# Third expert layer of a GNN and mixture-of-experts kernel: 512-column products with both weight halves, two running sums a token, bias terms on GpSimd

## The chip, the cores and the metric

The kernel runs on one core of a Trainium2 chip. The metric is the device time of one execution in microseconds (us). Before the change three runs gave 3012.4 us as the median (3011.11 to 3012.64).

## What is computed

A graph layer is followed by a dense mixture of eight experts over all 6250 rows of 256 features. The change touches only the second part, and in it the last product:

```python
h = jnp.einsum('bfd,edh->bfeh', x, W1) + b1
h = jax.nn.relu(_bn(h, g1, be1, m1, v1))
h = jnp.einsum('bfeh,ehk->bfek', h, W2) + b2
h = jax.nn.relu(_bn(h, g2, be2, m2, v2))
y = jnp.einsum('bfeh,ehd->bfed', h, Wo) + bo
return jnp.einsum('bfed,fe->bfd', y, w)      # w: softmax over the 8 experts
```

Every row goes through every expert. Products are done in split form: each operand is a rounded high half (fp32r) and a low half, and high x high, low x high and high x low are summed.

## The kernel before, in words

A first part (about 2110 us) normalizes, gathers 200000 edges, takes a segment maximum and runs the graph layer's products. The expert part follows. It has 7 chunks (c) of 7 token tiles (t) of 128 rows, and 8 experts (e) a chunk: 56 steps, n = 8c + e, written out one after another.

TensorE runs L2(n), L1(n+1), L3(n) in a step, so that what follows L3(n) is L2(n+1). L1 and L2 (lines 202 to 204) have the weights as the stationary operand and write a block m of 896 columns (a 512 and a 384 piece) into PSUM banks 0 and 1 (m = 0) or 2 and 3 (m = 1). ScalarE evacuates each block: `av` with scale, bias and Relu (line 1707), then the rounded copy `h1h` or `h2h` (line 1709). VectorE subtracts the two to get the low half, `low` (line 1846), which has two SBUF inputs. L2 waits until both blocks of `h1l` are there, L3 until both of `h2l` are there.

L3 (products on lines 2024 to 2026) has the tokens as the stationary operand. For each token tile and each of the two k blocks it does three products of 256 columns: h2h x high weights, h2l x high weights, h2h x low weights. Four token pairs go in turn to banks 4 and 5, so pair i waits until VectorE has read pair i-2.

VectorE runs its work in a hand-written order. Its part of L3 is `weighted` (line 1854): y = ps * w + y, 256 elements for each of 7 token tiles. `biased` (line 1841) adds the bias row times the weight: y = bo * w + y, also 7 a step, with both tensor inputs in SBUF. Chunk c+1 is prepared meanwhile: transposes on TensorE (lines 1928, 1939), `x_one`, `measure`, `norm`, `norm_lo`, router logits (`logits_in`, line 1819 on) and `softmax` on VectorE.

GpSimd has nothing in this part but one accumulating DMA a chunk (line 1648). SyncE issues the weights three steps ahead (`weights`), the chunk's residual rows and the output; the latter waits for `s_acc`, the count of `weighted` done.

## Time and profile before

| | us |
|---|---|
| median of three runs | 3012.4 |
| the profiled execution, its own time | 3013.89 |
| its span, first to last instruction | 3012.1 |
| expert part in the trace | about 2111 to 3012 |

The span is the time on the chip between the first and the last instruction that the profiler recorded; about 1.8 us of the execution's own time lie around it. Busy shares of the span are 93% for TensorE matmuls, 76% for VectorE, 65% for ScalarE, 49% for GpSimd, all of GpSimd's in the first part. A step of the expert part takes 14.84 us where nothing of the next chunk is prepared. A row of the timeline gives start, length, engine, line and operands; matmuls overlap, so the distance between two starts is their price, not the length.

### The profile page before, as it was taken

The numbers are of one execution on the slowest core, as the hardware profiler recorded it, in microseconds if no ns is written. First come the engines' busy times: TensorE is split into PE (matmuls) and PEld (weight loads), VectorE is DVE, ScalarE is ACT, GpSimd is POOL, SyncE is SP. The second block draws the span as 40 slices with busy tenths as digits, with TensorE's granted clock in tenths as the row PEclk, the third lists the DMA queues.
The fourth block names the chain that finished last, engine by engine and source line by source line (L and its number), as shares of the span: only waits on it lengthen the run. The fifth ranks groups of instructions, "written<-read, shape, count | busy, mean of one in ns | idle before, by whom it ended". The sixth has DMA issues, their size and how long they took to land. (4 is left out here: it accounts for less than half of the span.)

```text
span 3012.1 us, 40449 instructions
## 1 busy us (share of the span) xinstructions
PE 2796.6 (93%) x14193; PEld 2342.5 (78%) x14193; DVE 2292.7 (76%) x4785; ACT 1943.0 (65%) x2661; POOL 1484.6 (49%) x1550
## 2 busy tenths in 40 slices
PE   6699999999999999999999998789899999999998
PEld 6577777777776777777777777678799999999998
DVE  6887888888787888887878774498677677676766
ACT  5577777777777777777777765416465565655554
POOL 3677777777777777777777777631000000000000
PEclk9899999999999999999999999899899999999999
DMA  8577777777776666676666666411324334243231
GB/s 252 176 265 231 252 244 244 247 238 247 247 246 233 227 221 224 231 229 223 226 222 222 227 207 214 161 53 75 105 105 142 121 111 136 106 142 117 105 116 56
DMA packets 165632, 560.92 MB, mean 186 GB/s; under 512 B 31278, under 2 KB 68950, under 8 KB 149428
## 3 DMA queue, kind: packets, MB, share of 16 engines
q1 hardware_dynamic: 88164, 356.25, 32.9%
q0 software_dynamic: 77264, 202.08, 23.2%
q8 instruction: 112, 1.84, 0.2%
q14 instruction: 92, 0.75, 0.1%
HBM read 321.21 MB, written 237.00 MB: 185 GB/s over the span
## 5 line engine op out<-in xcount | busy, mean ns | idle before, releaser
L698 POOL DMA_INDIRECT ring<-runs,src_i x1436 | 1386.9, 966 | 469.1 <-issue 365.6
L1162 PE MATMUL ps<-oh,zhl 128*128 128x512 f32 x3136 | 1288.8, 411 | 115.7 <-ACT oh L727 103.4
L1164 PE MATMUL ps<-oh,zhl 128*128 128x512 f32 x3136 | 1245.4, 397 | 0.0
L914 DVE SCALAR_TENSOR_TENSOR ring<-ring,pen,ps 128x256 f32<-128x256 f32 x1260 | 598.8, 475 | 303.9 <-ACT ps L739 286.9
L1162 PEld LDWEIGHTS ps<-oh,zhl 128*128 128x128 f32 x3136 | 602.5, 192 | 284.8 <-ACT oh L727 130.6
L1164 PEld LDWEIGHTS ps<-oh,zhl 128*128 128x128 f32 x3136 | 602.8, 192 | 118.8
L921 DVE TENSOR_SCALAR oh<-ps,nodef 128x512 fp32r<-128x512 f32 x896 | 667.6, 745 | 0.0
L739 ACT ACTIVATE ps<-ring 128x512 f32<-128x512 f32 x630 | 370.4, 588 | 310.7 <-DMA ring<-runs,src_i 287.2
L721 ACT ACTIVATE oh<-ids,nodeneg 128x512 fp32r<-128x512 f32 x672 | 455.9, 711 | 27.0 <-PE ps L1164 26.9
L1707 ACT ACTIVATE av<-ps,vecs 128x896 f32<-128x896 f32 x224 | 246.4, 1100 | 325.3 <-PE ps L204 325.3
L727 ACT ACTIVATE oh<-oh,ones 128x1024 fp32r<-128x1024 f32 x448 | 414.7, 926 | 1.9
L1846 DVE TENSOR_TENSOR h2l<-av,h2h 128x896 fp32r<-128x896 f32 x112 | 122.2, 1092 | 148.4 <-ACT h2h L1709 148.1
L2024 PE MATMUL ps<-fw,h2h 128*128 128x256 f32 x784 | 224.5, 286 | 3.4 <-DVE h2l L1846 3.3
L2025 PE MATMUL ps<-fw,h2l 128*128 128x256 f32 x784 | 222.2, 283 | 0.0
L2026 PE MATMUL ps<-fw,h2h 128*128 128x256 f32 x784 | 222.0, 283 | 0.0
L1648 POOL DMA_DIRECT2D y<-in_x x5 | 8.4, 1685 | 412.1 <-DMA y<-res_d 412.1
L1854 DVE SCALAR_TENSOR_TENSOR y<-ps,wv,y 128x256 f32<-128x256 f32 x392 | 168.7, 478 | 52.6 <-PE ps L2026 52.5
L914 DVE SCALAR_TENSOR_TENSOR ring<-ring,pen 128x256 f32<-128x256 f32 x304 | 146.3, 481 | 76.0 <-DMA ring<-runs,src_i 70.9
L1841 DVE SCALAR_TENSOR_TENSOR y<-bo,wv,y 128x256 f32<-128x256 f32 x392 | 173.6, 479 | 1.4 <-issue 0.2
L202 PE MATMUL ps<-h1h,fw 128*128 128x512 f32 x448 | 168.0, 375 | 2.7 <-DVE h1l L1846 2.7
L203 PE MATMUL ps<-hnl,fw 128*128 128x512 f32 x448 | 164.7, 368 | 0.0
L204 PE MATMUL ps<-hnh,fw 128*128 128x512 f32 x448 | 164.6, 367 | 0.0
(294 smaller groups left out, 3976.1 us busy)
## 6 DMA issues: line engine op xcount, KB each, us to landing
runs<-ring SPq DMA_DIRECT2D x170, 768.0 KB, 3.9
fw<-wsp SPq DMA_DIRECT2D x56, 1536.0 KB, 6.5
runs<-ring SPq DMA_DIRECT2D x68, 1024.0 KB, 4.6
ring<-runs,src_i POOLq DMA_INDIRECT x1436, 3.7
ids<-srcT_d SPq DMA_DIRECT2D x32, 256.0 KB, 5.5
res_d<-x_all SPq DMA_DIRECT2D x7, 896.0 KB
y<-res_d SPq DMA_DIRECT2D x7, 896.0 KB, 8.1
part<-in_Wx SPq DMA_DIRECT2D x16, 384.0 KB, 7.1
```

Source lines behind the costliest of these rows:

```text
L698: pool.indirect_dma_start(ring[:, k, :], None, runs[0:N, :], bass.IndirectOffsetOnAxis(ap=src_i[:, STEPS * i + k:STEPS * i + k + 1], axis= ...
L721: return act.activation(oh[:, hot(i, g, v), :], ids[:, bass.ds(h, 1), :].rearrange("p a n -> p (a n)"), ACT.Abs, bias=nodeneg[:, bass.ds(S ...
L727: act.activation(oh[:, slots, :], oh[:, slots, :].bitcast(F32), ACT.Relu, bias=ones[:, 0:1], scale=-1.0).then_inc(s_oha, 1)
L739: act.activation(ps[:, RAWB[J % 2], :], ring[:, k:k + 2, :].rearrange("p s n -> p (s n)"), ACT.Copy).then_inc(s_cp, 1)
L914: dve.scalar_tensor_tensor(out=ring[:, k, :], in0=ring[:, before, :], scalar=pen[:, STEPS * i + k:STEPS * i + k + 1], in1=row, op0=ALU.add ...
L921: dve.tensor_scalar(oh[:, hot(i, g, v), :], ps[:, IDB, :], nodef[:, SLOTS * g + v:SLOTS * g + v + 1], None, ALU.is_equal).then_inc(s_ohd, 1)
L1162: pe.matmul(ps[:, two + k, :], z_hi(g)[:, v, cols], oh[:, hot(i, g, v), :], start=g == 0 and v == 0, stop=False, skip_group_check=True)
L1164: r = pe.matmul(ps[:, two + k, :], z_lo(g)[:, v, cols], oh[:, hot(i, g, v), :], start=False, stop=False, skip_group_check=True)
L1707: act.activation(av[:, m, :], block_banks(m), ACT.Relu, bias=dv(bi, 2 * e + m), scale=dv(sc, 2 * e + m)).then_inc(s_ev, 1)
L2024: pe.matmul(o, h2h[:, k, st], fw[:, b, 0, 2, k, :], start=k == 0, stop=False)
L2025: pe.matmul(o, h2l[:, k, st], fw[:, b, 0, 2, k, :], start=False, stop=False)
L2026: r = pe.matmul(o, h2h[:, k, st], fw[:, b, 1, 2, k, :], start=False, stop=k == KC - 1)
```

## The change

L3 does, for each token tile and k block, one product of 512 columns (h2h x high and low weights side by side, written to the two halves of a whole PSUM bank) and one of 256 columns (h2l x high weights, added to the first half). Seven tiles use banks 4, 5, 0, 1, 4, 2, 3. Banks 0 to 3 are shared with L1 and L2, so L3 waits for ScalarE's evacuation of them (`s_ev`), and L2 waits for VectorE's: block 0 until tiles 0 to 3 are read, block 1 until all 7 are.

`weighted` works on 512 elements in one instruction: first half into y[c % 3], second half into a new fourth buffer y[3]. The bias terms leave VectorE. GpSimd computes bo * w into y[3] (e = 0) or into `bw` (e > 0), and then adds `bw` to y[3] tile by tile, each add after the tile's `weighted` of the step before. At the end of a chunk GpSimd adds y[3] to y[c % 3] (`finished`), and the output DMA waits for that; in the last step VectorE does these adds (`finished_last`). GpSimd's accumulating DMA for chunk c+2 is issued after expert 2 of chunk c.

```diff
-                    for i, (t0, t1) in enumerate(PAIRS):
-                        if i >= 2:
-                            pe.wait_ge(s_acc, n * TPC + PAIRS[i - 2][1])
...
-                            for k in range(KC):
-                                pe.matmul(o, h2h[:, k, st], fw[:, b, 0, 2, k, :], start=k == 0, stop=False)
-                                pe.matmul(o, h2l[:, k, st], fw[:, b, 0, 2, k, :], start=False, stop=False)
-                                r = pe.matmul(o, h2h[:, k, st], fw[:, b, 1, 2, k, :], start=False, stop=k == KC - 1)
+                    for t in range(TPC):
+                        if t == 0 and n:
+                            pe.wait_ge(s_acc, (n - 1) * TPC + 5)
+                        if t == 2:
+                            pe.wait_ge(s_ev, 4 * first + 1)
+                        if t == 4:
+                            pe.wait_ge(s_acc, n * TPC + 1)
+                        if t == 5:
+                            pe.wait_ge(s_ev, 4 * first + 3)
+                        o = ps[:, OUTBANK[t], :].rearrange("p (a n) -> p a n", a=2)
+                        for k in range(KC):
+                            pe.matmul(o, h2h[:, k, st], fw[:, b, :, 2, k, :], start=k == 0, stop=False)
+                            r = pe.matmul(o[:, 0, :], h2l[:, k, st], fw[:, b, 0, 2, k, :], start=False, stop=k == KC - 1)
                         r.then_inc(s_l3, 1)
```
```diff
                 def L2(n):
                     pe.wait_ge(s_hl6, 4 * n + 2)
                     for m in range(KC):
+                        if n:
+                            pe.wait_ge(s_acc, (n - 1) * TPC + (4, TPC)[m])
                         layer(n, 1, m, h1h, h1l)
```
```diff
+                def biased(n, t):
+                    ...
+                    if e == 0:
+                        pool.tensor_scalar(y[:, 3, t, :], bo[:, 0, :], w, None, ALU.mult).then_inc(s_bi, 1)
+                    else:
+                        pool.wait_ge(s_bi, (n - 1) * TPC + t + 1)
+                        pool.tensor_scalar(bw[:, t, :], bo[:, e, :], w, None, ALU.mult).then_inc(s_bw, 1)
+                def add_biased(n, t):
+                    pool.wait_ge(s_bw, TPC * (n - c - 1) + t + 1)
+                    pool.wait_ge(s_acc, (n - 1) * TPC + t + 1)
+                    pool.tensor_tensor(y[:, 3, t, :], y[:, 3, t, :], bw[:, t, :], ALU.add).then_inc(s_bi, 1)
+                def finished(c, t):
+                    pool.wait_ge(s_acc, (NE * c + NE - 1) * TPC + t + 1)
+                    pool.tensor_tensor(y[:, c % 3, t, :], y[:, c % 3, t, :], y[:, 3, t, :], ALU.add).then_inc(s_fin, 1)
```
```diff
-                def weighted(n, i):
+                def weighted(n, t):
-                    dve.wait_ge(s_l3, n * NPAIR + i + 1)
-                    dve.wait_ge(s_bi, n * TPC + PAIRS[i][1])
+                    dve.wait_ge(s_l3, n * TPC + t + 1)
+                    dve.wait_ge(s_bi, n * TPC + t + 1)
+                    dve.scalar_tensor_tensor(out=both(c, t), in0=ps[:, OUTBANK[t], :].rearrange("p (a n) -> p a n", a=2),
+                                             scalar=wv[:, c % 2, t * NE + e:t * NE + e + 1], in1=both(c, t),
+                                             op0=ALU.mult, op1=ALU.add).then_inc(s_acc, 1)
```

VectorE's order in a step becomes: low h2l (two blocks), low h1l block 0, weighted 0 and 1, low h1l block 1, weighted 2 and 3, (expert 7: `logits_in`), weighted 4, 5, 6, then what prepares the next chunk. In the last step it is: weighted 0 to 3; then finished_last(t-4) and weighted(t) for t = 4, 5, 6; then finished_last 3 to 6.

## Rows read from the trace of the kernel before

**Rows 1.** The page, part 1: busy time, share of span, instructions.
```profile
PE 2796.6 (93%) x14193; PEld 2342.5 (78%) x14193; DVE 2292.7 (76%) x4785; ACT 1943.0 (65%) x2661; POOL 1484.6 (49%) x1550
```
**Rows 2.** Windows: stretch, its length, then PE, PEld, DVE, ACT, POOL busy, PEclk, DMA.
```profile
2430.00:2490.00 60.00, 60.00 (x372) 55.84 (x371) 43.79 (x85) 37.24 (x38) 0.00 (x0) 1.00 0.30 106
```
**Rows 3.** Waits, 2135 to 3013 us: who waited for whom, total, times, longest.
```profile
PE ps L202 <- DVE h1l L1846: 2.7, 1, 2.7
```
**Rows 4.** Groups by line and form, whole span: VectorE reading 512 elements from PSUM.
```profile
L921 DVE TENSOR_SCALAR oh<-ps,nodef 128x512 fp32r<-128x512 f32 x896 | 667.6, 745 | 0.0
```
**Rows 5.** Timeline, TensorE, one plain step of the last chunk: start, length, operation.
```profile
2941.42 0.28 PE L2024 MATMUL ps<-fw,h2h 128*128 128x256 f32 x1
...
2946.44 0.47 PE L202 MATMUL ps<-h1h,fw 128*128 128x512 f32 x1
2946.75 0.40 PE L203 MATMUL ps<-h1l,fw 128*128 128x512 f32 x1
...
2951.40 0.39 PE L202 MATMUL ps<-hnh,fw 128*128 128x512 f32 x1
...
2952.79 0.33 PE L202 MATMUL ps<-hnh,fw 128*128 128x384 f32 x1
```
**Rows 6.** Timeline, VectorE, the same step, L3 and the start of L2.
```profile
2941.35 1.09 DVE L1846 TENSOR_TENSOR h1l<-av,h1h 128x896 fp32r<-128x896 f32 x1 [0.55 <-ACT h1h L1709]
...
2944.49 0.88 DVE L1854 SCALAR_TENSOR_TENSOR y<-ps,wv,y 128x256 f32<-128x256 f32 x2 [0.46 <-PE ps L2026]
2945.28 1.08 DVE L1846 TENSOR_TENSOR h1l<-av,h1h 128x896 fp32r<-128x896 f32 x1
2946.28 1.26 DVE L1854 SCALAR_TENSOR_TENSOR y<-ps,wv,y 128x256 f32<-128x256 f32 x3
```
**Rows 7.** Timeline, TensorE, the start of L2 in the second step.
```profile
2157.12 0.40 PE L202 MATMUL ps<-h1h,fw 128*128 128x512 f32 x1
2157.36 0.40 PE L203 MATMUL ps<-h1l,fw 128*128 128x512 f32 x1
```
**Rows 8.** Timeline, VectorE, just before that start.
```profile
2155.70 1.08 DVE L1846 TENSOR_TENSOR h1l<-av,h1h 128x896 fp32r<-128x896 f32 x1
```
**Rows 9.** Timeline, ScalarE, the step of rows 5: the second block's high half.
```profile
2942.80 0.95 ACT L1709 ACTIVATE h1h<-av 128x896 fp32r<-128x896 f32 x1
```
**Rows 10.** Timeline, GpSimd in the first 30 us: next to VectorE, and alone.
```profile
18.54 0.76 POOL L414 TENSOR_SCALAR x_all<-x_all,fine 128x256 f32<-128x256 f32 x1 [1.38 <-DVEq L490]
...
19.28 1.10 POOL L414 TENSOR_SCALAR x_all<-x_all,fine 128x256 f32<-128x256 f32 x1
...
21.05 3.99 POOL L426 TENSOR_TENSOR x_all<-x_all,h0c 128x1792 f32<-128x1792 f32 x1
27.59 0.56 POOL L414 TENSOR_SCALAR x_all<-x_all,fine 128x256 f32<-128x256 f32 x1 [2.56 <-DVEq L490]
```
**Rows 11.** Timeline, VectorE in the same microseconds.
```profile
18.23 0.17 DVE L489 SCALAR_TENSOR_TENSOR fine<-fine 128x7 f32<-128x7 f32 x1
...
18.66 0.29 DVE L539 CAST b1h<-b1r 128x256 fp32r<-128x256 f32 x1
18.86 0.58 DVE L540 TENSOR_SCALAR bb<-b1r,ident 128x256 fp32r<-128x256 f32 x1
19.36 0.67 DVE L542 TENSOR_TENSOR w1l<-w1r,w1h 128x512 fp32r<-128x512 f32 x1
...
20.68 2.02 DVE L495 TENSOR_TENSOR h0l<-ps,h0h 128x1792 fp32r<-128x1792 f32 x1
```
**Rows 12.** Timeline, VectorE, a step of expert 7: the router logits.
```profile
2514.01 0.27 DVE L1819 TENSOR_REDUCE wv<-ps 128x56 f32<-128x112 f32 x1
...
2514.79 1.26 DVE L1854 SCALAR_TENSOR_TENSOR y<-ps,wv,y 128x256 f32<-128x256 f32 x3
```
**Rows 13.** Timeline, VectorE, the end of the last step.
```profile
3003.89 0.88 DVE L1854 SCALAR_TENSOR_TENSOR y<-ps,wv,y 128x256 f32<-128x256 f32 x2 [0.56 <-PE ps L2026]
3005.32 1.27 DVE L1854 SCALAR_TENSOR_TENSOR y<-ps,wv,y 128x256 f32<-128x256 f32 x3 [0.56 <-PE ps L2026]
```

More of the change, by code:

```diff
@@ L1596, in build, with both @@
         LAST = NCH - 1
[L1597 to L1598 removed]
+        OUTBANK = (4, 5, 0, 1, 4, 2, 3)
+        def both(c, t):
+            return y[:, c % 3:4:3 - c % 3, t, :]
         def cols67(n):
@@ L1644, in _, with plus_input @@
                 pool.memset(br[:], 0.0).then_inc(s_z, 1)
-                for c in range(1, NCH):
+                def plus_input(c):
                     pool.wait_ge(s_res[c % 3], 16 * (c // 3 + 1))
@@ L1653, in _ @@
                         pool.dma_start(y[0:TAIL, c % 3, TPC - 1, :], io["x"][N - TAIL:N, :], accum_op=ALU.add).then_inc(s_rx[c % 3], 16)
+                def biased(n, t):
+                    c, e = divmod(n, NE)
+                    w = wv[:, c % 2, t * NE + e:t * NE + e + 1]
+                    if e == 0:
[4 more added lines that the diff above has]
+                def add_biased(n, t):
+                    c, e = divmod(n, NE)
+                    pool.wait_ge(s_bw, TPC * (n - c - 1) + t + 1)
[4 more added lines that the diff above has]
+                    pool.tensor_tensor(y[:, c % 3, t, :], y[:, c % 3, t, :], y[:, 3, t, :], ALU.add).then_inc(s_fin, 1)
+                plus_input(1)
+                plus_input(2)
+                pool.wait_ge(s_bo, 16)
+                for c in range(NCH):
+                    if c:
+                        pool.wait_ge(s_fin, TPC * c)
+                    pool.wait_ge(s_w, c + 1)
+                    for e in range(NE):
+                        for t in range(TPC):
+                            biased(NE * c + e, t)
+                        if e:
+                            for t in range(TPC):
+                                add_biased(NE * c + e, t)
+                        if e == 2 and 1 <= c < NCH - 2:
+                            plus_input(c + 2)
+                    if c < NCH - 1:
+                        for t in range(TPC):
+                            finished(c, t)
             def block_banks(m):
@@ L1832, in softmax @@
                     dve.drain()
-                def biased(n, t):
-                    c, e = divmod(n, NE)
-                    if n == 0 and t == 0:
-                        dve.wait_ge(s_bo, 16)
-                    if e:
-                        dve.wait_ge(s_acc, (n - 1) * TPC + t + 1)
-                    yt = y[:, c % 3, t, :]
-                    dve.scalar_tensor_tensor(out=yt, in0=bo[:, e, :], scalar=wv[:, c % 2, t * NE + e:t * NE + e + 1], in1=yt,
-                                             op0=ALU.mult, op1=ALU.add).then_inc(s_bi, 1)
                 def low(l, m, hi, lo):
@@ L1884, in _ @@
                         softmax(0)
-                        for t in range(3):
-                            biased(n, t)
-                    biased(n, 3)
-                    biased(n, 4)
                     if e == 1 and c < LAST:
@@ L1892, in _ @@
                         low(2 * n + 2, 0, h1h, h1l)
-                    biased(n, 5)
-                    biased(n, 6)
                     weighted(n, 0)
@@ L1898, in _ @@
                         low(2 * n + 2, 1, h1h, h1l)
+                    weighted(n, 2)
+                    weighted(n, 3)
+                    if e == 7 and c < LAST:
+                        logits_in(c + 1)
+                    if more:
+                        weighted(n, 4)
+                        weighted(n, 5)
+                        weighted(n, 6)
+                    else:
+                        for t in range(4, TPC):
+                            finished_last(t - 4)
+                            weighted(n, t)
+                        for t in range(3, TPC):
+                            finished_last(t)
                     if c < LAST:
@@ L1903, in _ @@
                             norm_lo(c + 1, e - 4)
-                        if e == 7:
-                            logits_in(c + 1)
-                    weighted(n, 2)
-                    weighted(n, 3)
-                    if c < LAST:
                         if e == 1:
```

40 lines of the change are left out of this document (16 added, 24 removed).

## The prediction, as it was made before the changed kernel ran

> **What bounds the kernel now.** I read the busy shares first, then the expert part by windows, then TensorE's waits, then the timeline of one step engine by engine. TensorE is busy for 93% of the span [rows 1]; in a window inside the expert part it is busy 60.00 of 60 us at a granted clock of 1.00, the 2.4 GHz level, while VectorE has 43.8 us of work and GpSimd none [rows 2]. From 2135 us on the list of waits has one entry for an L2 product, 2.7 us [rows 3]. So the expert part costs what TensorE's stream costs, and only two things can move it: a cheaper stream, or a new wait in it.
>
> One wait hides from that list. In the plain step L2's first product starts at 2946.44 and its second at 2946.75, 0.31 us later [rows 5]. At 2157 us the same two are 0.24 us apart [rows 7]. The difference is when VectorE's `low` of the second h1l block ends: at 2156.78 in the one [rows 8], 0.34 us ahead of L2, and at 2946.36 in the other [rows 6], 0.08 us ahead. The product really starts about 0.08 us later than its row shows. I write S for the start of L3, X for the free start of L2 and E for the end of the VectorE instruction that L2 waits for. With E = X - 0.08 giving a loss of 0.08, the loss is E + 0.16 - X where that is positive. Before, it is 0.08 us in nearly all steps: the same 0.08 lies between `low` and L2 at each of the 30 or so L2 starts that I compared after the first.
>
> **The stream.** L3 takes 2946.44 - 2941.42 = 5.02 us for 42 products, 0.1195 us each [rows 5]. Six products of 512 columns take 2952.79 - 2951.40 = 1.39 us, 0.2317 each [rows 5]. The new L3 has 14 of each: 14 x (0.2317 + 0.1195) = 4.92 us. Columns are unchanged; only 14 starts go. The stream saves 0.10 us a step, about 5.7 us in all. It is small, and any new wait of 0.1 us a step eats it. The Trainium skill (TensorE: Matmul & The Clock Gate, Back-to-back issue gap) gives columns / 2.4 GHz plus 2.5 ns for a product alone, by which only 0.035 us a step would be saved and my sum would end 3.7 us higher; the 0.2317 us of the trace is above its 0.216, so I go by the trace.
>
> **VectorE in a step.** It loses 7 `biased` and its 7 `weighted` double. Three of 256 elements last 1.26 us with 0.48 for the last, so one starts 0.39 us after another [rows 6]; 256 elements more at one each VectorE cycle add 0.27: 0.66 us apart, 0.745 long, the length that a 512-element read of PSUM has [rows 4]. Total work falls by 7 x (0.39 + 0.39 - 0.66) = 0.8 us, which is worth nothing by itself. What matters is the order. Now L2 must wait for `weighted` 0 to 3, not only for `low`.
>
> In the plain step `low` block 0 starts at S - 0.07 [rows 6] and takes 1.00 us before the next can start (2945.28 to 2946.28 [rows 6]), so VectorE is free at S + 0.94. Tile 0 leaves TensorE at about S + 0.89: its last product starts at 0.58, and the second pair's products, the last starting at 23 x 0.1195 = 2.75, were followed by `weighted` at 3.07 [rows 5, 6], 0.32 later. Weighted 0 runs 0.94 to 1.69, weighted 1 starts 1.60. The high half of block 1 is there at 2943.75 = S + 2.33 [rows 9], so `low` block 1 wants to start at 2.37. Then weighted 2 at 3.38, weighted 3 at 4.04, ending 4.79. Loss: 4.79 + 0.16 - 4.92 = 0.03. By VectorE's order alone the change would halve the loss, not add to it. The margin is nil, though: what delays this chain by 0.1 us costs 0.1 us a step.
>
> **GpSimd, and the port.** GpSimd's add for tile 0 follows weighted 0. A release by VectorE takes 0.14 us (18.40 to 18.54 [rows 10, 11]), so it starts at S + 1.83. The trace has no add of 256 elements. Bounds: not below the one-input 0.56 us of 27.59 [rows 10]. Above: the 1792-element add takes 3.99 [rows 10]; if 0.34 of it is start-up, a rate of 2.04 ns an element gives 0.86; the slowest one-input instruction, held up, took 1.10 [rows 10]. I take 0.86, since it is the same operation: S + 1.83 to 2.69. That lies across 2.37, where `low` with two SBUF inputs wants to start.
>
> Do they share something? From 18.5 to 21 us they meet. GpSimd's 0.56 us instruction took 0.76 and 1.10 us [rows 10], and VectorE's 256-element instruction 0.58, where the one before it took 0.29 [rows 11]. The 512-element subtraction with two SBUF inputs took its normal 0.67 while the GpSimd instruction that had started 0.08 us earlier stretched to 1.10. In contrast the 1792-element subtraction with one input in PSUM took 2.02 next to the 3.99 us add [rows 10, 11], about one element a cycle. So two-input SBUF work on VectorE and GpSimd's reading exclude each other, and the later one waits for the rest of the earlier one; `weighted`, with PSUM, is free of it. This is also what the Trainium skill says (SBUF — State Buffer, Who interferes with whom): an exclusive lock against GpSimd for VectorE instructions with two SBUF inputs. It speaks against moving just this add to GpSimd, and the trace agrees with 0.29 to 0.58 and 0.56 to 1.10, except that the row that started first did not always win.
>
> So `low` block 1 waits until about S + 2.66; the next add starts up while `low` runs, and yields. Then E = 2.66 + 2.42 = 5.08, loss 0.32. L3 and wait: 4.92 + 0.32 = 5.24 against 5.02 + 0.08 = 5.10 before: +0.14 us for 25 steps (experts 1 to 3 of six chunks and seven steps of the last). In the 30 steps with transposes or logits between L1 and L3, VectorE is free for `low` at 2.25, tile 0 starts at 0.89 and everything ends 0.03 earlier: +0.11. Sum 25 x 0.14 + 30 x 0.11 = +6.8 us. Bounds: with an add of 0.56 the same reckoning gives 25 x -0.13 + 30 x -0.17 = -8.4; with 1.10, +0.24 a step more, +20.
>
> Its other work fits. Seven adds of 0.86 and seven products of 0.54 (the row at 27.59 less a little overlap) are 9.8 us plus up to 3 us of yielding, of 14.9. The adds must be done by the next step's S + 0.9 and are by about S + 8.8. `low` of h2l meets the products, delayed up to 0.5 us, but L3 needs it 1 us or more later. The accumulating DMA costs GpSimd under 2 us after expert 2's adds, when nothing waits; its rows are needed a chunk's end later. The output DMA leaves about 1 us later behind `finished`, and the weights queued behind it on SyncE are three steps ahead. TensorE's new waits on ScalarE are for tile 2 at S + 1.4 and tile 5 at S + 3.5. The high copy of block 1 starts at S + 1.38 [rows 9], so its evacuation is done by then and block 0's half an L2 (2.4 us [rows 5]) earlier. Tile 4, at S + 2.8, has weighted 0 from 1.69.
>
> **Expert 7.** `logits_in` takes 2514.79 - 2514.01 = 0.78 us [rows 12] and now stands ahead of weighted 4 to 6, for which L2's block 1 waits. E of weighted 6 = 2.63 + 1.00 + 6 x 0.66 - 0.66 - 0.66 + 0.78 + 0.745 = 7.80; block 1 would start at 5.21 + 2.43 = 7.64. Loss 0.32, six times: +1.9 us. In other steps weighted 6 ends at 7.05, in time.
>
> **The end.** Before, three `weighted` from 3005.32 close the work at 3006.59 [rows 13]. Now VectorE alternates: weighted 3 at about 3004.0 is followed by add (0.34), weighted 4 at 5.0, add, weighted 5 at 6.0, add, weighted 6 at 7.0, then four adds from 3007.7, ending near 3009.1. +2.5 us, nothing hides it.
>
> **Sum.** +6.8 + 1.9 + 2.5 = +11.2; the saved 0.10 us a step is in it. Against the profiled execution's 3013.9 (span 3012.1 and 1.8 around it) that is 3025.1; the median of the runs lies 1.5 lower, so 3023.6.
>
> **Rivals.**
> 1. *The port does not bite* (chance 0.20): the add is short, or reads early and frees `low` by 2.4. Sum -8.4 + 1.9 + 2.5 = -4.0: 3008. For it: the 0.67 us subtraction was not delayed. Against: GpSimd's start at 1.83 plus even 0.56 passes 2.37.
> 2. *Faster beyond doubt* (0.12): as 1, and L2 starts free of any loss with a tail half as long, as when the queue runs ahead behind 0.23 us products; -55 x 0.18 and +3 give 3005. It decides where weighted 3 ends before S + 4.76.
> 3. *GpSimd goes twice* (0.08): the second add, released at 2.35, takes the port before `low`. Another 0.86 us in 55 steps: 3070. Against: in [rows 10, 11] VectorE got in between two GpSimd instructions.
> 4. *The wide product or the wide `weighted` is dearer* than its row (0.10): two segments of 256 in place of one run, unseen in the trace. `weighted` at 0.745 apart adds 0.09 a step, +5; 0.02 us on each of 14 products adds 15 us: 3030 to 3040.
> The forecast has 0.50.
>
> The range reaches from rival 1 to rival 4: 3006.5 to 3038. About 0.2% (6 us) is what a measurement of this kernel can tell from no change. Below 3006.4: 0.12. Within: rival 1 and the forecast's lower edge, 0.26. Above: 0.62.
>
> **What would show it.** Right: L2's first two products 0.5 us apart or its row late, with `low` block 1 starting near S + 2.65, not 2.37; `low` rows of block 1 longer than 1.09; a 512-column product of L3 every 0.351 us; `weighted` 0.745 long; a new entry of TensorE waiting for y at line 202. Wrong: `low` starting at 2.37 next to a GpSimd add, GpSimd adds under 0.5 us, or L3 longer than 4.95 us from first to last.

## The result, and the profile of the changed kernel

The changed kernel takes 3018.96 us (3015.12 to 3024.85) against 3012.64 (3010.72 to 3016.5) before, medians of 17 runs each: a ratio of 1.002, 95% interval 1.0013 to 1.0026. It is 6.3 us slower, that is by the 0.2% that can just be told from no change, and 4.6 us below the forecast. The profiled execution is 3021.28 us long (span 3019.4) against 3013.89.

The page of the changed kernel, busy time of each engine, then a window table of it, columns as in [rows 2], over the 760 us in which the stages repeat most evenly (parts of chunks 0 to 6); the third line is the same window of the kernel before:

```profile
PE 2786.3 (92%) x13409; PEld 2287.2 (76%) x13409; DVE 2292.7 (76%) x4400; ACT 1939.7 (64%) x2661; POOL 2216.6 (73%) x2327
```
```profile
2180.00:2940.00 760.00, 747.86 (x3910) 648.58 (x3910) 545.81 (x731) 436.99 (x436) 655.92 (x689) 1.00 0.35 118
```
```profile
2180.00:2940.00 760.00, 760.00 (x4660) 700.18 (x4659) 550.98 (x1084) 447.65 (x445) 7.41 (x5) 1.00 0.36 119
```

TensorE, which before was busy for all of this window, now stands for 12.1 us of it, at the same granted clock of 1.00. Its waits there (total, times, longest; the kernel before has none) are these:

```profile
PE ps L202 <- DVE y L1884: 7.0, 12, 0.9
PE ps L2063 <- DVE h2l L1878: 4.0, 5, 1.1
```

The first is the new wait of L2 for `weighted` that the prediction named as a sign. Eleven of its twelve come at the L2 products that follow the steps of experts 1 and 4, not at those of the plain steps. The second is L3 waiting for `low` of h2l. GpSimd went from 7 to 656 us of 760. VectorE has hardly less to do than before: 546 us in place of 551. (The trace merges what overlaps, so a group's busy time is less than the sum of its lengths.)

**Where the time went.** I call the time from the first L2 product to the end of the last VectorE instruction the expert part, and measure each of its 56 steps from L2's start to the next L2's start. Step 0 and the last step vary from run to run in every kernel (16.4 to 19.1 us and 13.4 to 16.2). In the last step TensorE is at times at a lower level: the kernel before has a granted clock of 0.88 in 2992 to 3001 us and 1.00 in 3003 to 3005. Steps 1 to 54 are steadier, 833.7 to 833.9 us in three executions of the kernel before, and the verdicts rest on them.

| | before | after | change |
|---|---|---|---|
| first L2 product at | 2138.88 | 2130.60 | -8.3 |
| step 0 | 18.24 | 17.95 | -0.3 |
| steps 1 to 54 | 833.9 | 846.7 | +12.8 |
| last step | 14.72 | 14.89 | +0.2 |
| from the last product to the end | 0.87 | 3.31 | +2.4 |
| expert part | 867.7 | 882.8 | +15.1 |

So the small total hides two larger numbers: the expert part became 15.1 us longer, and the part ahead of it, which the diff doesn't touch, 8.3 us shorter.

The 12.8 us don't lie in the plain steps. Those went from 14.85 to 14.75 us. The steps of expert 4 cost 9.1 us more (15.74 each before; now 16.69, 17.29, 17.30, 18.19, 18.19, 15.94 for chunks 0 to 5), those of expert 1 2.0 more and that of the last chunk another 2.1, those of expert 0 after a new chunk's logits 1.9, step 2 0.4. That is 15.5; the other steps, 0.05 to 0.15 us shorter each, give back 2.7.

TensorE in the plain step that answers to [rows 5], timeline (start, length, engine, line, operation, operands); left out are the rows from 2441.45 to the last product of L3:

```profile
2441.11 0.39 PE L2063 MATMUL ps<-fw,h2h 128*128 128x512 f32 x1
2441.33 0.28 PE L2064 MATMUL ps<-fw,h2l 128*128 128x256 f32 x1
2441.45 0.39 PE L2063 MATMUL ps<-fw,h2h 128*128 128x512 f32 x1
...
2445.84 0.28 PE L2064 MATMUL ps<-fw,h2l 128*128 128x256 f32 x1
2446.03 0.47 PE L202 MATMUL ps<-h1h,fw 128*128 128x512 f32 x1
2446.33 0.40 PE L203 MATMUL ps<-h1l,fw 128*128 128x512 f32 x1
```

L3 takes 2446.03 - 2441.11 = 4.92 us, a pair of products about 0.35, as forecast. L2's first product is followed by its second 0.30 us later, 0.31 in [rows 5]: the hidden loss of 0.08 us is still there, no larger, though by VectorE's order alone I had 0.03. VectorE and GpSimd in the same step, which answer to [rows 6]:

```profile
2441.04 1.09 DVE L1878 TENSOR_TENSOR h1l<-av,h1h 128x896 fp32r<-128x896 f32 x1 [1.34 <-ACT h1h L1751]
2442.05 1.40 DVE L1884 SCALAR_TENSOR_TENSOR y<-ps,wv,y 128x512 f32<-128x512 f32 x2
2443.47 1.09 DVE L1878 TENSOR_TENSOR h1l<-av,h1h 128x896 fp32r<-128x896 f32 x1
2444.48 3.38 DVE L1884 SCALAR_TENSOR_TENSOR y<-ps,wv,y 128x512 f32<-128x512 f32 x5
```

The second `low` starts at 2443.47 = S + 2.36, where I had its free start, and has its normal 1.09 us. The five `weighted` take 3.38, so (3.38 - 0.745) / 4 = 0.66 from one to the next, as forecast. The collision that was to hold `low` didn't come here, since GpSimd is late: its first add starts at 2443.80. One step further it came, GpSimd first and VectorE second:

```profile
2460.17 0.74 POOL L1672 TENSOR_TENSOR y<-y,bw 128x256 f32<-128x256 f32 x1 [2.19 <-DVE y L1884]
2460.87 1.58 POOL L1672 TENSOR_TENSOR y<-y,bw 128x256 f32<-128x256 f32 x1
```
```profile
2460.60 1.26 DVE L1878 TENSOR_TENSOR h1l<-av,h1h 128x896 fp32r<-128x896 f32 x1
```

`low` lost 1.26 - 1.09 = 0.17 us and the second add gave way: 1.58 us from its start to its end, where an undisturbed one takes 0.74.

**What holds TensorE.** The groups of GpSimd and VectorE in the expert part (columns: busy us, mean ns | idle before), and then two of its lines by themselves (shortest/median/longest ns):

```profile
L1666 POOL TENSOR_SCALAR bw<-bo,wv 128x256 f32<-128x256 f32 x343 | 387.3, 1323 | 0.0
L1672 POOL TENSOR_TENSOR y<-y,bw 128x256 f32<-128x256 f32 x343 | 279.0, 935 | 44.1 <-DVE y L1884 44.0
L189 DVE TENSOR_TENSOR fine<-fine 128x7 f32<-128x7 f32 x6 | 11.5, 1922 | 0.4
```
```profile
L1666 POOL TENSOR_SCALAR bw<-bo,wv x343: 915/934/3131, 2149.5 to 2989.6; 128x256 f32<-128x256 f32 x172
```
```profile
L1672 POOL TENSOR_TENSOR y<-y,bw x343: 723/743/2361, 2156.2 to 2997.3; 128x256 f32<-128x256 f32 x172
```

The product takes 0.93 us when nothing disturbs it and 1.32 on average; I had put it at 0.54. The add takes 0.74, less than my 0.86. Seven of each are 11.7 us alone and 15.8 by the means (less what overlaps), of a step's 15. GpSimd is never waiting at the product (0.0 us idle before it): it runs behind, and a late start is made up only by doing seven products and then seven adds without a gap. The group in line 189 shows who pays. It is one instruction of 7 elements a partition in the norm of the next chunk, and took 1922 ns on average. The step of expert 4 in chunk 3, GpSimd's timeline:

```profile
2562.98 8.98 POOL L1666 TENSOR_SCALAR bw<-bo,wv 128x256 f32<-128x256 f32 x7
2571.93 4.91 POOL L1672 TENSOR_TENSOR y<-y,bw 128x256 f32<-128x256 f32 x7
```

and VectorE's in the same stretch, with ScalarE's evacuation that follows:

```profile
2573.74 3.12 DVE L189 TENSOR_TENSOR fine<-fine 128x7 f32<-128x7 f32 x1
...
2578.31 3.29 DVE L1848 TENSOR_SCALAR hn<-y,fine 128x256 f32<-128x256 f32 x7
2581.53 2.27 DVE L1878 TENSOR_TENSOR h2l<-av,h2h 128x896 fp32r<-128x896 f32 x2
```
```profile
2582.70 1.10 ACT L1749 ACTIVATE av<-ps,vecs 128x896 f32<-128x896 f32 x1 [3.69 <-DVE h2l L1878]
```

VectorE's instruction starts 1.8 us into GpSimd's row of adds and ends at 2576.86, when the seventh add ends (2571.93 + 4.91 = 2576.84). What is queued behind it on VectorE comes late: the last five norm instructions, `hn`, for which TensorE's transposes wait, and then `low` of h2l, for which L3 and, over ScalarE's evacuation (3.69 us idle), the rest of the stream wait. The transposes of that step take 2.20 us in place of 0.79 and L3 6.06 in place of 5.12. After expert 1 it is `low` of h2l itself that meets a row of seven adds (2403.35 to 2408.27):

```profile
2405.39 5.15 DVE L1878 TENSOR_TENSOR h2l<-av,h2h 128x896 fp32r<-128x896 f32 x2 [1.99 <-ACT h2h L1751]
```

5.15 us for two where 2.1 would do, and the step is 15.95 us long in place of 15.52.

**The head.** The gather ahead of the expert part issues 1436 indirect DMAs on GpSimd, one behind the other. Their line before, and after:

```profile
L698 POOL DMA_INDIRECT ring<-runs,src_i x1436: 952/957/1670, 89.4 to 1912.5; - x180
```
```profile
L698 POOL DMA_INDIRECT ring<-runs,src_i x1436: 945/949/1807, 91.1 to 1906.5; - x180
```

The median is 8 ns less, and 1436 x 8 ns = 11.5 us, enough for the 8.3 us by which the first L2 product comes earlier. The line and all ahead of it are the same in both kernels.

### The profile page after: what moved, and what is told of

Same layout as the page of the kernel before. It is cut to its first block and busy times, and to the rows that moved or that the text cites. A ratio compares the mean times of both kernels' runs of the same rounds, so it can differ in the third digit from the quotient of the medians.

```text
span 3019.4 us, 39846 instructions
## 1 busy us (share of the span) xinstructions
PE 2786.3 (92%) x13409; PEld 2287.2 (76%) x13409; DVE 2292.7 (76%) x4400; ACT 1939.7 (64%) x2661; POOL 2216.6 (73%) x2327
## 5 line engine op out<-in xcount | busy, mean ns | idle before, releaser
L1666 POOL TENSOR_SCALAR bw<-bo,wv 128x256 f32<-128x256 f32 x343 | 387.3, 1323 | 0.0
L1672 POOL TENSOR_TENSOR y<-y,bw 128x256 f32<-128x256 f32 x343 | 279.0, 935 | 44.1 <-DVE y L1884 44.0
L2063 PE MATMUL ps<-fw,h2h 128*128 128x512 f32 x784 | 279.4, 398 | 7.5 <-DVE h2l L1878 7.4
L1884 DVE SCALAR_TENSOR_TENSOR y<-ps,wv,y 128x512 f32<-128x512 f32 x392 | 269.6, 741 | 21.9 <-PE ps L2064 21.8
L1878 DVE TENSOR_TENSOR h2l<-av,h2h 128x896 fp32r<-128x896 f32 x112 | 145.8, 1310 | 157.2 <-ACT h2h L1751 156.5
L1878 DVE TENSOR_TENSOR h1l<-av,h1h 128x896 fp32r<-128x896 f32 x112 | 128.2, 1145 | 73.1 <-ACT h1h L1751 72.3
L2063 PEld LDWEIGHTS ps<-fw,h2h 128*128 128x128 f32 x784 | 147.7, 188 | 41.3 <-DVE h2l L1878 9.3
L202 PE MATMUL ps<-h1h,fw 128*128 128x512 f32 x448 | 168.1, 375 | 11.5 <-DVE y L1884 7.7
```

Of the source, the lines that this page charges most:

```text
L202: pe.matmul(out, wh, xh, start=first and i == 0, stop=False)
L1666: pool.tensor_scalar(bw[:, t, :], bo[:, e, :], w, None, ALU.mult).then_inc(s_bw, 1)
L1884: dve.scalar_tensor_tensor(out=both(c, t), in0=ps[:, OUTBANK[t], :].rearrange("p (a n) -> p a n", a=2), scalar=wv[:, c % 2, t * NE + e:t * ...
L2063: pe.matmul(o, h2h[:, k, st], fw[:, b, :, 2, k, :], start=k == 0, stop=False)
```

## Experiments

Two theories first. *Load and row*: after is slow because GpSimd has both products and adds and is behind, and because its adds run back to back and hold VectorE. *Rival*: the wide `weighted` and the new order on VectorE are to blame, and GpSimd's part is cheap. On the chip of the first four runs the part ahead took some 570 us more in every kernel, before's too (first L2 product at 2711 to 2724; GpSimd waits 540.4 us for VectorE's ring there, 71.6 here), so of these runs the expert part is compared. Their whole times show nothing of what is gained in it: the kernels without the bias work, with the products only and with the adds only took 1.0017 (0.9998 to 1.0036), 1.0015 (0.9999 to 1.0031) and 1.0024 (1.0007 to 1.0041) of the kernel before there.

**The kernel before again**, unchanged.

> The kernel before, profiled a second time, to see what repeats. The expert part (first L2 product to the last VectorE instruction) took 867.7 us before and 882.8 us after, +15.1, while the part ahead of it was 8.3 us shorter after (first L2 product at 2130.6 us against 2138.9), although the change does not touch it. Theory A (the build is what differs): GpSimd's indirect DMA instruction, median 957 ns in the kernel before and 949 ns after, shows 957 ns again and the first L2 product comes at 2137 to 2140 us. Theory B (chance of one execution): the first L2 product comes anywhere from 2128 to 2140 us and the indirect DMA's median moves with it. The expert part should repeat within 0.5 us under both.

The indirect DMA has 957 ns again, on another chip. The first L2 product comes at 2714, which neither theory had. Steps 1 to 54 repeat, 833.7 us, but the expert part, 866.3, is 1.4 less than 867.7 and not within the 0.5 that I expected; step 0 (16.77 in place of 18.25) accounts for it.

**No bias work after expert 0.** Leaves out the biases of experts 1 to 7, so `weighted` waits for GpSimd at expert 0 alone.

```diff
-                    for e in range(NE):
-                        for t in range(TPC):
-                            biased(NE * c + e, t)
-                        if e:
-                            for t in range(TPC):
-                                add_biased(NE * c + e, t)
...
+                    for t in range(TPC):
+                        biased(NE * c, t)
```

> Left out: the bias terms of experts 1 to 7 (GpSimd's products and adds); the rest of the change stays, so what is left is the wide product, the wide weighted, the banks, the router logits ahead of weighted 4 to 6 and the longer end. Port theory: the 15.1 us of the expert part come from GpSimd; without it L3 falls to 4.93 us in every step, the step of expert 4 to about 15.6 us (16.7 to 18.2 with it), and the expert part takes 867.7 - 5.7 (stream) - 2.8 (wait ahead of L2) + 2.6 (logits) + 2.4 (end) = 864 us. Rival (the wide product or the wide weighted is what costs): the expert part stays near 883 us.

Steps 1 to 54: 828.8 us, expert part 861.9 (864 expected), 4.4 less than the kernel before on that chip (866.3). All of the 12.8 us and 5 more go with GpSimd's work. Of the steps of expert 4 none is over 15.65.

**Products only.** Each bias is multiplied, nothing is added (experts 1 to 7 lack their bias).

```diff
-                        pool.wait_ge(s_bi, (n - 1) * TPC + t + 1)
-                        pool.tensor_scalar(bw[:, t, :], bo[:, e, :], w, None, ALU.mult).then_inc(s_bw, 1)
+                        pool.wait_ge(s_acc, (n - 1) * TPC + t + 1)
+                        pool.tensor_scalar(bw[:, t, :], bo[:, e, :], w, None, ALU.mult).then_inc(s_bi, 1)
```

> Left out: the bias adds of experts 1 to 7; GpSimd still computes the products of bias and weight, each released by weighted of the step before. Starvation theory: VectorE with two SBUF inputs is held up for long only by back-to-back GpSimd adds, which themselves read two tensors; against products it waits for less than one. Expert part 865 to 868 us. Rival (any GpSimd work costs in proportion to its time, products being the longer ones): about half of the excess or more is left, 873 us and up.

828.5 us, as with no bias work at all: expert part 862.9, below the 865 to 868 that I expected. The products as such, one input in SBUF, cost nothing. Line 189 takes 0.48 us beside them in all six places.

**Adds only.** The products are done for expert 0 alone, the adds add a block of zeros.

```diff
-                    pool.wait_ge(s_bw, TPC * (n - c - 1) + t + 1)
+                    pool.wait_ge(s_bw, 1)
```

> Left out: the bias products of experts 1 to 7; GpSimd adds a buffer set to zero once. Theory (the two together make GpSimd late, and late adds run back to back without waiting for weighted): alone, the adds follow weighted and end some 8 us into the step; VectorE's norm of the next chunk meets the last of them, so the step of expert 4 keeps at most 1 us of its excess of 1 to 2.5 and the step of expert 1 nothing: expert part 866 to 870 us. Rival (the adds alone carry the cost, whatever their lateness): 878 us and up. In the plain steps low of the second h1l block waits for the first add, 0.1 to 0.3 us, in both.

832.8 us, expert part 867.2: the adds alone cost 4.0 us, not 18. GpSimd now idles before its adds, each waiting for the `weighted` of its tile, and line 189 takes 0.18 us in all six places. The group of these adds:

```profile
L1670 POOL TENSOR_TENSOR y<-y,bw 128x256 f32<-128x256 f32 x332 | 275.4, 859 | 395.9 <-DVE y L1883 394.9 <-issue 0.9
```

In this kernel the collision of the forecast happens in the plain steps, on time. L3 starts at 3110.67; VectorE's second `low` of h1l, and GpSimd beside it:

```profile
3113.04 1.15 DVE L1877 TENSOR_TENSOR h1l<-av,h1h 128x896 fp32r<-128x896 f32 x1
```
```profile
3112.50 2.29 POOL L1670 TENSOR_TENSOR y<-y,bw 128x256 f32<-128x256 f32 x2 [9.46 <-DVE y L1883]
```

The add starts at S + 1.83 and `low` at S + 2.37, both as forecast, but `low` loses only 0.06 us (1.15 in place of 1.09) where I had 0.29, and it is the second add that is stretched. L3 takes 4.99 us here and 4.93 without bias work: 0.06 us a step, 3.2 of the 4.0 if all 54 steps lose as much.

So no part of GpSimd's work does it by itself: none 828.8, products 828.5, adds 832.8, both 846.7. Since the products alone cost nothing and the adds alone are on time, I read the other 14 us as the price of adds that the products have made late.

**`logits_in` behind weighted 6** (everything else as in the changed kernel).

```diff
-                    if e == 7 and c < LAST:
-                        logits_in(c + 1)
                     if more:
...
                         weighted(n, 6)
+                        if e == 7 and c < LAST:
+                            logits_in(c + 1)
```

> The changed kernel with logits_in after weighted 6 in place of after weighted 3. If the 0.42 us by which L2 is longer in the steps that follow expert 7 (5.38 against 4.96 us) comes from weighted 6 being late, L2 goes back to 4.96 there and steps 1 to 54 lose 2.5 us (846.7 to about 844.2). If it comes from GpSimd's adds of finished, it stays 5.38.

844.5 us, 2.1 less, and the L2 in expert 0's steps is back from 5.38 us to the 4.96 of before, six times 0.42, where the forecast had 0.32. (The steps of expert 4 take 2.1 us more in this execution and those of expert 1 less, so the total shows it only roughly.) VectorE's timeline in the changed kernel and in this one:

```profile
2510.41 0.26 DVE L1861 TENSOR_REDUCE wv<-ps 128x56 f32<-128x112 f32 x1
2511.34 0.74 DVE L1884 SCALAR_TENSOR_TENSOR y<-ps,wv,y 128x512 f32<-128x512 f32 x1
```
```profile
2503.35 3.37 DVE L1884 SCALAR_TENSOR_TENSOR y<-ps,wv,y 128x512 f32<-128x512 f32 x5
2506.64 0.26 DVE L1861 TENSOR_REDUCE wv<-ps 128x56 f32<-128x112 f32 x1
```

**Biases back on VectorE**, fused as before, but into the second half of the wide sum; the wide product and the wide `weighted` stay.

```diff
+                    if n:
+                        biased(n, 0)
                     low(2 * n + 1, 0, h2h, h2l)
+                    if n:
+                        biased(n, 1)
+                        biased(n, 2)
+                        biased(n, 3)
                     low(2 * n + 1, 1, h2h, h2l)
```

> The product and weighted as in the changed kernel, but the bias terms and finished on VectorE: the change without GpSimd. VectorE then has 4.4 + 7 x 0.66 + 7 x 0.39 = 11.7 us of work in a step of 14.75, with biased placed ahead of the low of h1l, where it had been idle. If GpSimd is the only thing that costs: plain steps 14.75 us, steps 1 to 54 in 828 to 830 us (833.8 before), end 3.3 us as in the changed kernel. Rival (VectorE becomes late, since finished adds 2.4 us after expert 7 and biased 6 stands ahead of low): 835 us and up, with steps of expert 0 above 16.3.

827.2 us, 6.7 less than the kernel before and a little under what I expected, expert part 864.2. TensorE is busy for 760.00 of the 760 us again. In all, 3005.49 against 3008.66, a ratio of 0.9989 (0.998 to 0.9998). The wide product is worth its 0.1 us a step and a little more, once nothing waits.

**Narrow product, biases on GpSimd.** The other half: three products of 256 columns and `weighted` of 256, with GpSimd's products and adds as in the changed kernel.

```diff
-                            pe.matmul(o, h2h[:, k, st], fw[:, b, :, 2, k, :], start=k == 0, stop=False)
-                            r = pe.matmul(o[:, 0, :], h2l[:, k, st], fw[:, b, 0, 2, k, :], start=False, stop=k == KC - 1)
+                            pe.matmul(o[:, 0, :], h2h[:, k, st], fw[:, b, 0, 2, k, :], start=k == 0, stop=False)
+                            pe.matmul(o[:, 0, :], h2l[:, k, st], fw[:, b, 0, 2, k, :], start=False, stop=False)
+                            r = pe.matmul(o[:, 0, :], h2h[:, k, st], fw[:, b, 1, 2, k, :], start=False, stop=k == KC - 1)
```

> The changed kernel with the products and weighted of the kernel before (three of 256 columns, 256 elements), everything else as changed: GpSimd's part alone. If the wide form saves 0.10 us a step and costs nothing, plain steps take 14.85 to 14.95 us and L3 5.02 at the least. With VectorE faster in weighted (2.7 us against 4.6 us) L2's wait for tiles 0 to 3 goes, but GpSimd is as late as before, so the steps of experts 1 and 4 keep their excess of 0.4 and 1 to 2.5 us: steps 1 to 54 take 845 to 852 us. If the wide form is what makes VectorE late, they fall to 836 us or less.

I had expected 845 to 852 and got 834.3, 0.4 more than before. Yet VectorE is held here as long as in the changed kernel, or longer. Its instruction of line 189 in the step where expert 4 begins, timeline and group:

```profile
2562.26 3.19 DVE L189 TENSOR_TENSOR fine<-fine 128x7 f32<-128x7 f32 x1
```
```profile
L189 DVE TENSOR_TENSOR fine<-fine 128x7 f32<-128x7 f32 x6 | 14.1, 2350 | 0.4
```

Expert 4's steps are 15.66, 16.35, 16.37, 16.37, 17.26 and 15.67: 3.2 us more than before in sum, where the changed kernel has 9.1. In chunk 3 the norm begins 0.60 us after L2's start here, 1.01 in the kernel before and 1.75 in the changed one; its `weighted` of 0.74 in place of 0.48 us bring VectorE to the norm late already, and the hold comes on top. The rest of the 3.2 us is given back by the plain steps (14.78, L2 4.89 in place of 4.97: the hidden loss of 0.08 is gone, where VectorE has neither the biases nor the wide `weighted`). So the cost is an interaction: the wide form without GpSimd -6.7, GpSimd's work without the wide form +0.4, both +12.8. The whole time of the one execution was 3004.07 us, 5.8 below the 3009.88 of the kernel before on that chip, though its expert part was 1.4 longer than that kernel's (870.3 against 868.9): the part ahead was shorter again (first L2 product at 2125.97 against 2134.37).

**Product and add by turns.** The changed kernel with its two loops over the tiles made one, so that no add directly follows another.

```diff
-                        if e:
-                            for t in range(TPC):
+                            if e:
                                 add_biased(NE * c + e, t)
```

> Nothing is left out: GpSimd does the same 343 products and 343 adds as in the changed kernel, but in the order product 0, add 0, product 1, add 1 and so on, so that no two adds run back to back. In the changed kernel seven adds in a row held a VectorE instruction with two SBUF inputs until the last had ended (2573.74 to 2576.86 us next to adds from 2571.93 to 2576.84). Train theory (VectorE gets in only where GpSimd does something other than an add next): the step of expert 4 falls from 17.3 to 18.2 us to 16 or less, that of expert 1 from 15.95 to 15.5, and steps 1 to 54 take 830 to 835 us in place of 846.7. Load theory (the total of GpSimd's reading is what costs): 843 us and up, since the load is the same. Each product now waits behind an add that weighted releases, so low of the second h1l block may meet the first add: up to 0.3 us a step under both.

841.5 us: 5.2 of the 12.8 are gone, between the two expectations, so neither holds alone. Ratio 1.0003 (0.9994 to 1.0013). GpSimd and VectorE in one such step:

```profile
2441.15 0.74 POOL L1672 TENSOR_TENSOR y<-y,bw 128x256 f32<-128x256 f32 x1
2441.87 0.92 POOL L1666 TENSOR_SCALAR bw<-bo,wv 128x256 f32<-128x256 f32 x1
```
```profile
2441.32 0.60 DVE L189 TENSOR_TENSOR fine<-fine 128x7 f32<-128x7 f32 x1
2443.72 4.02 DVE L1847 TENSOR_SCALAR hn<-y,fine 128x256 f32<-128x256 f32 x7
```

The hold is now to the end of one add, 0.60 us in place of 3.12. But the seven `hn` take 4.02 us, where the kernel with the biases on VectorE has 2.35 and the changed one 3.29: what the row no longer costs, contact with a never idle GpSimd partly costs again. Expert 4's steps are still 16.75 us in three chunks.

**A row of GpSimd instructions in the kernel before.** Nothing else on GpSimd; in each chunk, where the norm's work begins, seven instructions of 256 elements back to back into a buffer nobody reads, adds in chunks 0, 2, 4 and 6, products (one input) in chunks 1, 3 and 5.

```diff
+                def burst(c):
+                    pool.wait_ge(s_acc, (NE * c + 3) * TPC + 5)
+                    pool.wait_ge(s_bw, 1 + TPC * c)
+                    for t in range(TPC):
+                        if c % 2:
+                            pool.tensor_scalar(bw[:, 1, t, :], bo[:, t, :], 2.0, None, ALU.mult).then_inc(s_bw, 1)
+                        else:
+                            pool.tensor_tensor(bw[:, 1, t, :], bw[:, 0, t, :], bo[:, t, :], ALU.add).then_inc(s_bw, 1)
```

> The kernel before, with seven idle GpSimd instructions of 256 elements put once a chunk beside VectorE's norm of the next chunk: released by weighted of tile 4 in the step of expert 3, in chunks 0, 2 and 4 two-input adds, in chunks 1, 3 and 5 one-input products; their results are not used. Train theory: the seven-element VectorE instruction at line 189, which has two SBUF inputs and takes 0.17 us alone, is held until the last add of the row has ended, 3 us or more, in chunks 0, 2 and 4, and next to the products it takes under 1 us. Rival (VectorE waits for at most the one GpSimd instruction under way, whatever its kind): under 0.8 us in all six. The step of expert 4, 15.74 us, grows by 1 to 2 us after adds and by 0 to 0.3 us after products.

834.3 us, 0.4 more than before. Expert 4's steps are 16.00 us after adds and 15.73 after products (15.74 before). The row of adds and two of VectorE's instructions beside it:

```profile
2196.87 4.96 POOL L1658 TENSOR_TENSOR bw<-bw,bo 128x256 f32<-128x256 f32 x7 [76.04 <-DVE y L1872]
```
```profile
2197.75 0.57 DVE L189 TENSOR_TENSOR fine<-fine 128x7 f32<-128x7 f32 x1
2198.40 0.61 DVE L191 SCALAR_TENSOR_TENSOR fine<-fine 128x7 f32<-128x7 f32 x1
```

Both end while the row still runs. VectorE got in once an add, and was held 0.4 us each time, not until the row's end. "A row of adds keeps VectorE out until it is over" is thereby refuted as a rule. It happens in the changed kernel and in the one with the narrow product, not here.

The length of line 189 in chunks 0 to 5 over the kernels:

| kernel | us, chunk 0 to 5 |
|---|---|
| after | 0.41, 2.16, 2.17, 3.12, 3.04, 0.64 |
| after, second time | 0.34, 2.16, 2.17, 3.12, 3.94, 0.62 |
| logits late | 0.48, 3.12, 3.12, 3.12, 3.04, 0.17 |
| narrow product | 0.17, 3.19, 3.19, 3.19, 4.07, 0.29 |
| by turns | 0.32, 0.59, 0.60, 0.58, 0.32, 0.32 |
| products only | 0.48 in all |
| adds only | 0.18 in all |
| row in the kernel before | 0.57, 0.42, 0.58, 0.38, 0.58, 0.37 |

Two things suggest themselves as what decides: how long after an add's start VectorE's instruction comes (0.14 to 0.18 us in the last kernel), and that the last kernel's adds write a buffer of their own, the others y. The traces speak against both. In the second profile of the changed kernel, chunk 0, VectorE and GpSimd:

```profile
2191.19 0.34 DVE L189 TENSOR_TENSOR fine<-fine 128x7 f32<-128x7 f32 x1
```
```profile
2189.37 4.93 POOL L1672 TENSOR_TENSOR y<-y,bw 128x256 f32<-128x256 f32 x7
```

Line 189 starts 1.82 us into the row of seven adds and is held to the end of one add, 0.34 us. In chunk 3 of the first profile it starts 1.81 us into an equal row (2571.93 to 2573.74), with adds that write the same y, and is held for 3.12. The same with `low` of h2l after expert 1, where the first of the two in chunk 2 lost 2.77 us (3.86 in place of 1.09), 2.04 us into the row. Chunk 3, also 2.04 us into its row:

```profile
2531.54 1.73 DVE L1878 TENSOR_TENSOR h2l<-av,h2h 128x896 fp32r<-128x896 f32 x1 [1.99 <-ACT h2h L1751]
```
```profile
2529.50 6.62 POOL L1672 TENSOR_TENSOR y<-y,bw 128x256 f32<-128x256 f32 x7
```

It lost 0.64. So neither the moment nor the buffer decides alone, and what does is open. Being held is not confined to two inputs either: line 193, with one, takes 0.63 us at 2192.30 beside the adds of that chunk 0, 0.17 alone.

**The best version.** The kernel with biases on VectorE, `logits_in` behind weighted 6, and a last step of its own: the halves of y are joined ahead of it, and it uses three products of 256 and a `weighted` of 256.

```diff
+                    if not more:
+                        for t in range(TPC):
+                            dve.wait_ge(s_bi, n * TPC + t + 1)
+                            yt = y[:, c % 3, t, :]
+                            dve.tensor_tensor(yt, yt, y[:, 3, t, :], ALU.add).then_inc(s_finl, 1)
...
-                    L3(n)
+                    if n + 1 < STEPN:
+                        L3(n)
+                    else:
+                        L3_last(n)
```

> As e5, with logits_in after weighted 6, and the last step with three products of 256 columns and the second sum folded in ahead of it, so that the end is that of the kernel before. Expected: steps 1 to 54 in 826 to 828 us, last step and end as before (15 and 0.9 us), expert part 8 us shorter than before, ratio 0.997 to 0.998 to the kernel before. Rival as for e5: no gain, ratio 1.000.

2999.66 us against 3008.66, a ratio of 0.9972 (0.9961 to 0.9983): faster than both by a few tenths of a per cent, as expected. Steps 1 to 54 825.8, expert part 858.1, 9.6 less than before, of which 8.1 lie in steps 1 to 54 and 1.7 in step 0, which varies. The end, VectorE's timeline: the seven joins are done 3.3 us before the last `weighted`, and the work ends 0.79 us after the start of the last product.

```profile
2986.16 2.43 DVE L1921 TENSOR_TENSOR y<-y 128x256 f32<-128x256 f32 x7
...
2991.92 0.48 DVE L1872 SCALAR_TENSOR_TENSOR y<-ps,wv,y 128x256 f32<-128x256 f32 x1 [0.23 <-PE ps L2085]
```

**Both kernels once more**, on a third chip, for the head.

> The changed kernel once more. Its steps of expert 4 took 15.9 to 18.2 us in one execution, which would be chance in how GpSimd and VectorE meet; the sum of steps 1 to 54 should come out at 844 to 849 us again. The indirect DMA instruction should have a median of 949 ns, as it had, if its length belongs to the build, and the first L2 product should come about 8 us ahead of that of the kernel before on the same chip.

> The kernel before on the same chip as the changed kernel's second profile, for the part ahead of the expert part: indirect DMA instruction 957 ns, first L2 product 7 to 9 us later than in the changed kernel, steps 1 to 54 in 833.8 us.

After: steps 1 to 54 848.0 us, first L2 product at 2121.22, whole time 3015.12, ratio 1.0017 (1.0008 to 1.0027). Before: 833.8, 2134.37 and 3010.56. The line of indirect DMAs, first before and then after:

```profile
L698 POOL DMA_INDIRECT ring<-runs,src_i x1436: 949/953/1746, 91.1 to 1909.2; - x180
```
```profile
L698 POOL DMA_INDIRECT ring<-runs,src_i x1436: 942/946/1778, 91.4 to 1898.1; - x180
```

7 ns each are 10 us of the 13.1 by which the changed kernel's first L2 product is earlier. It repeats in kind, but 13.1 is more than the 7 to 9 that I expected and the medians are 946 and 953 in place of 949 and 957. That the shorter instructions make the product come earlier is likely, not shown: on the chip of the first four runs, where GpSimd mostly waited for VectorE, the kernels with 946 to 949 ns had their first L2 product at 2711 to 2724, the kernel before with 957 at 2714. Over all runs the median is 946 to 949 ns in the seven kernels in which GpSimd has bias work, 953 in the two with the biases on VectorE and in the one with the added row, 957, 957 and 953 in the kernel before. The instruction and its operands are the same in all. What moves it is open.

## Why the prediction held, and which of its steps did not

The number and the sign came out (forecast +11.2 us, measured +6.3, range 3006.5 to 3038), but only half by the steps that I wrote.

- *The stream*: right. 4.92 us for L3 in place of 5.02, a pair of products 0.35, and with the biases on VectorE steps 1 to 54 fell by 6.7 us in all. The rule of the Trainium skill (TensorE: Matmul & The Clock Gate, Back-to-back issue gap) for a product alone, by which only 0.035 us a step would go, is further off than the rows: L3 fell by 0.10.
- *VectorE's order*: right in its times, 0.66 from one `weighted` to the next and `low` of block 1 free to start at S + 2.36. The loss ahead of L2 stayed at 0.08, where I had it fall to 0.03.
- *The port at `low` of block 1*, +6.8 us: wrong, and it was the main term. The meeting exists, but `low` does not wait for the rest of the add. In the kernel with adds only, where it comes exactly at S + 2.37, it costs 0.06 us in place of 0.29; in the changed kernel 0.17 (2460.60), and nothing in the steps where GpSimd is behind. Adds are 0.74, not 0.86, and the second one gives way. The plain steps are 0.10 us shorter, not 0.14 longer, and `low` starting at 2.37 next to an add was my own sign of being wrong. That is the outcome of rival 1, to which I gave 0.20, but for another reason than its short add: the add is late. The reading behind the term was weak too. In [rows 11] I set VectorE's 0.58 against 0.29 as the price of the port, but the one is a product with a scalar and the other a cast, neither has two SBUF inputs, and the one two-input row there, 0.67, was not delayed.
- *"Its other work fits"*, taken at nothing: this is the other step that failed, and the one that cost the time. I read the product from the row of 0.56 us in [rows 10], an instruction with two operations and one input; it is 0.93 alone and 1.32 on average. Seven of each then take all of a step. GpSimd falls behind at each chunk's start (14 products in a row) and at the DMA after expert 2, and its adds come in rows late in the step, where VectorE does the next chunk's norm and `low` of h2l. I said of that `low` that it would be delayed by up to 0.5 us, with 1 us in hand; it was up to 3.7 us in the first profile (4.82 in place of 1.09 in the last chunk's expert 1) and 4.6 in the second. The runs without adds (828.5), without products (832.8), without either (828.8) and with both (846.7) show that it takes both, and the narrow product (834.3) that it takes the wide form as well, which brings VectorE to the norm 1.75 us after L2's start in place of 0.60.
- *Expert 7*: right in kind and nearly in size, 0.42 us of L2 a chunk against 0.32, and 2.1 us in all against 1.9 when undone.
- *The end*: right. +2.44 against +2.5. VectorE adds and `weighted` by turns, and then four adds close it:

```profile
3011.32 0.75 DVE L1884 SCALAR_TENSOR_TENSOR y<-ps,wv,y 128x512 f32<-128x512 f32 x1
3011.99 1.42 DVE L1891 TENSOR_TENSOR y<-y 128x256 f32<-128x256 f32 x4
```

- *The part ahead of the expert part*: taken as unchanged, 8.3 us shorter. Without it the change would have shown as some 15 us, above the forecast.

Added up in expert-part terms: +12.8 and +2.4 were measured, where I had +8.7 and +2.5. That the terms' errors partly cancelled, and that the head then gave 8 us back, is luck.

The Trainium skill (SBUF — State Buffer, Who interferes with whom) calls the shared port pair an exclusive lock and says that whoever issues first gets it for the whole instruction, while the other fully blocks. The hold of one instruction agrees with 0.57 and 0.60 us of line 189 beside adds of 0.74. The row at 3113.04 does not: an add had started 0.54 us earlier and had 0.20 to go, and `low` lost 0.06. A hold over four or five adds, as at 2573.74, goes beyond what it states.

## What to carry to other kernels

Work moved to a second engine must be priced by that engine's own instruction in the same form (one operation with a per-row scalar, here 0.93 us, is not the two-operation one of 0.56), and summed over a step: near a full load it will be late, and the question is then not whether it collides where you planned it, but whom its late and bunched instructions meet. Look in each stage for the neighbour's two-input SBUF work and for the slack that the same change takes from it; two edits that are harmless alone (+0.4 and -6.7 us) cost 12.8 together. And when a total moves by a few microseconds, split it by stage before explaining it: here +15.1 and -8.3 made it up.

## What the runs showed that I had not expected

- A VectorE instruction of 7 elements, 0.17 us alone, was held for 2.16 to 4.07 us beside back-to-back adds of GpSimd in three kernels and only 0.57 us beside an equal row in another; in the changed kernel itself it was held for 0.34 and for 3.12 us at the same place in an equal row. What decides is open.
- The same indirect DMA instruction takes 946 to 957 ns by the median in different builds, 7 to 11 ns less with bias work on GpSimd than without on the same chip, some 10 us or more over 1436 of them. A build moves by up to 4 ns between chips (957 for the kernel before on two of three chips, 953 on the third).
- GpSimd's product of 256 elements with a scalar of each row: 0.93 us; the add of two inputs, 0.74.
